# GpSimd's product of the states with C: one instruction for the three units of a group in place of three

## The chip, the cores and the metric
The kernel runs on one core of a Trainium2 chip. The metric is device time in microseconds (us), the median of some runs. The engines are named as the profile names them: PE (TensorE; PEld its weight loads), DVE (VectorE), ACT (ScalarE), POOL (GpSimd) and SP (SyncE, which only issues DMAs here).

## What is computed
Sixteen images of 64x64 positions with 96 channels pass two layers, each added to its input: first an upsampling, two matrix products around a quadratic and a downsampling, then a selective scan over the 4096 positions of each image:

```python
dA  = jnp.exp(delta[..., None] * A)                  # 192 inner channels x 16 states
dBu = delta[..., None] * Bm[:, :, None, :] * xc[..., None]
def step(h, inp):
    dA_t, dBu_t, C_t = inp
    h = dA_t * h + dBu_t
    y = jnp.einsum('bdn,bn->bd', h, C_t)             # the states times C, summed over the states
    return (h, y)
y = ys + xc * D
y = y * silu(z)                                      # and then the output projection
```

Before each layer stands a group normalization, whose sums need the whole image.

## The kernel before
**Units, groups, chunks.** The 192 x 16 pairs of channel and state of an image are laid out as 24 units of 128 rows, and the 4096 positions as 8 chunks of 512 columns. Three units that share their four states make a group, so a chunk has 8 groups, an image 64, and the program 1024. The text writes group 3/6 for group 6 of chunk 3 of an image, counting from zero.

**One group goes round the engines.** PE spreads B over the rows into the single PSUM bank `pb` (`spread_b`, L847). DVE multiplies `rep_u` with it (L1135 for two units, L1138 for the third) and runs three scans, one for each unit, into `hs` (L1145). ACT has made their factors `av` (L1009). POOL multiplies each unit's states `hs` with C, `cs`, into `hc` (L1186), and after the third copies the last column of the three states to `state` (L1190), where the next chunk's scans begin. PE then sums `hc` over the states into `py` (`reduce`, L856, six matmul records); ACT copies `py` out (L1052) once for four groups. `hs` and `hc` hold six units, two groups. DVE's first scan of a group waits for the copy of two groups before (`pool_st`), and POOL's first product for PE's reduction of two groups before (`pe_red`).

**What else POOL does in a chunk.** Two additions and products on `xcs` (L1235, L1238), two subtractions that split B in bf16 parts (L1211 to `dbc`, L1215 to `bc`), and one product of two 512-column halves on `dlt` (L1223), which waits for a DMA that stores `dlt` first. They stand at unit counts given by `AT["pool"]`, each behind the unit's product where one stands. Small steps of the normalization (L1173, L1176) stand among them.

**The order around it.** Everything is written out by hand: each engine walks the same unit counts, with a lag for some (`LAG`). On PE, between the units, stand the steps of the other layer for later images (`level`, `even`) and the projections of the scan (`X` L811, `Z` L817, `DBC`, `DT`, `OUT`). `spread_b` of group g+1 stands at unit 3g+1, and `reduce` of group g at 3g+5, behind `spread_b` of group g+2 and ahead of that of g+3. Where PE has little to do, `warm` puts in matmuls without a use (L711). Fourteen images run the full plan of steps (one first and thirteen full), the last two a plan with less and less on PE. PE waits in `reduce` on the semaphore `pool_hc`, of which POOL raises one for each product:

```python
pe.wait_ge(pool_hc, count(pool_hc, G * NU + 3 * g + 3))   # NU = 24 units, NG = 8 groups a chunk
```

Of the kernel before, what the change touches and what calls it, by code (L numbers as in the profile page):

```python
# [9 lines left out]
ALU = mybir.AluOpType  # L10
# [11 lines left out]
T = 512  # L22
NC8 = L // T
NJ, NQ = DI // 32, DSTATE // 4
NU = NJ * NQ
NG = NU // 3
NHC, NAV, NHS = 6, 8, 6
XB_H = 8
LEAD = 2
# [6 lines left out]
AT = {  # L36
    "pe": dict(pb=1, red=5),
    "act": dict(xn=10, y=(18, 6), d=11, mid=23, batch=16),
    "dve": dict(),
    "pool": dict(u=23, bc=(18, 22), y=(17, 8)),  # L40
    "sp": dict(rd=(1, 2, 3, 4), ru=(7, 9, 11, 13), cs=(15, 16, 17, 18), dl=21, du=4, x1=21, out=23),
}
# [155 lines left out]
def build(nc, A):  # L198
    ctx = ExitStack()
    with ctx:  # L200
        def sb(name, shape, dt=F32):
            return ctx.enter_context(nc.sbuf_tensor(name, shape, dt))
# [4 lines left out]
        def sem(name):  # L207
            return ctx.enter_context(nc.semaphore(name))
# [77 lines left out]
        cs = sb("cs", [128, 2, NQ, T])  # L286
        av = sb("av", [128, NAV, T])
        hs = sb("hs", [128, NHS, T])
        hc = sb("hc", [128, NHC, T])
# [6 lines left out]
        state = sb("state", [128, NG, 3])  # L296
# [53 lines left out]
        pool_st = sem("pool_st")  # L350
        pool_hc = sem("pool_hc")
        pe_red = sem("pe_red")
# [21 lines left out]
        def tok(ap, s, t0_, n):  # L374
            v = ap[bass.ds(s, 1), t0_:t0_ + n, :].rearrange("o t c -> (o t) c")
            return v.rearrange("(i p) c -> p i c", p=128)
# [107 lines left out]
        def count(sm, v):  # L484

            return max(v, 0)

        def ahead(s, k):

            return (s, k + LEAD) if k + LEAD < NC8 else (s + 1, k + LEAD - NC8)  # L490
# [4 lines left out]
        def _(sp):  # L495
# [112 lines left out]
            def load_x1o(s, k):  # L608

                src = x1_d[bass.ds(s, 1), :, k * T:(k + 1) * T].rearrange("o c t -> (o c) t")  # L610
                sp.dma_start(x1o[:, :], src).then_inc(x1o_ld, 16)
# [20 lines left out]
            def c_part(st, k, n):  # L632
                G = st.s * NC8 + k
                at = AT["sp"]
                if not ((G < -1 or G + 1 >= NS * NC8)):

                    p = (k + 1) % 2
                    if n == at["du"]:
                        sp.wait_ge(pool_u, count(pool_u, G + 2))
                        sp.sem_inc(sp_passed, 1)  # L640
                        sp.dma_start(du_d[p].rearrange("(t p) f -> p t f", p=C), dlt[:, :, :]).then_inc(du_st, 16)
                    if n == at["rd"][0]:
                        sp.wait_ge(dl_st, count(dl_st, (G + 2) * 16))
                        sp.sem_inc(sp_passed, 1)
                        sp.wait_ge(act_a, count(act_a, G * NU))
                        sp.sem_inc(sp_passed, 1)
                    if n == at["ru"][0]:
                        sp.wait_ge(du_st, count(du_st, (G + 2) * 16))
                        sp.sem_inc(sp_passed, 1)
                        sp.wait_ge(dve_bu, count(dve_bu, G * NG))  # L650
                        sp.sem_inc(sp_passed, 1)
                    if n == at["cs"][0]:
                        sp.wait_ge(dc_st, count(dc_st, (G + 2) * 16))
                        sp.sem_inc(sp_passed, 1)
                        sp.wait_ge(pool_hc, count(pool_hc, G * NU))
                        sp.sem_inc(sp_passed, 1)
                    for r in range(4):
                        rows = slice(32 * r, 32 * r + 32)
                        if n == at["rd"][r]:
                            sp.dma_start(rep_d[rows, p], dl_d[p].rearrange("(j p) f -> p j f", p=32))\  # L660
                                .then_inc(rd_ld[p], 16)
                        if n == at["ru"][r]:
                            sp.dma_start(rep_u[rows, p], du_d[p].rearrange("(j p) f -> p j f", p=32))\
                                .then_inc(ru_ld[p], 16)
                        if n == at["cs"][r]:
                            src = dc_d[p].rearrange("(q r) f -> r q f", r=4)[r].partition_broadcast(32)
                            sp.dma_start(cs[rows, p], src).then_inc(cs_ld[p], 16)
                if n == at["out"] and not (G < 1):
                    i = st.at[("OUT", k)]
                    sp.wait_ge(cb_free[i % RING], st.freed(i))  # L670
                    sp.sem_inc(sp_passed, 1)
                    k1, s1 = (k - 1) % NC8, st.s + (k - 1) // NC8
                    sp.dma_start(tok(otok, s1, k1 * T, T), os_[:, :, :]).then_inc(out_st, 16)
                if n == at["out"] and k < NC8 and not (G < 0):

                    load_x1o(st.s, k)
# [13 lines left out]
        def _(pe):  # L690
# [158 lines left out]
            def reduce(s, k, g):  # L849
                G = s * NC8 + k  # L850
                hf, q = g // NQ, g % NQ
                pe.wait_ge(pool_hc, count(pool_hc, G * NU + 3 * g + 3))
                if q == 0:
                    pe.wait_ge(act_y, count(act_y, G * 2 + hf))
                for j in range(3):
                    mm = pe.matmul(py[32 * j:32 * j + 32, :], rsel[:, :], hc[:, (3 * g + j) % NHC, :],  # L856
                                   start=(q == 0), stop=(q == NQ - 1), skip_group_check=True)
                mm.then_inc(pe_red, 1)
# [292 lines left out]
        def _(pool):  # L1151
# [26 lines left out]
            def unit(s, k, n):  # L1178
                G = s * NC8 + k
                g = n // 3  # L1180
                if n == 0:
                    pool.wait_ge(cs_ld[k % 2], count(cs_ld[k % 2], s * (4 * 64) + (k // 2 + 1) * 64))
                if n % 3 == 0:
                    pool.wait_ge(pe_red, count(pe_red, G * NG + g + 1 - NHC // 3))
                pool.wait_ge(dve_h, count(dve_h, G * NU + n + 1))
                pool.tensor_tensor(hc[:, n % NHC, :], hs[:, n % NHS, :], cs[:, k % 2, g % NQ, :], ALU.mult)\  # L1186
                    .then_inc(pool_hc, 1)
                if n % 3 == 2:

                    pool.tensor_copy(state[:, g, :], hs[:, n % NHS - 2:n % NHS + 1, T - 1]).then_inc(pool_st, 1)  # L1190

            def a_part(st, k, n):
                if n in AT["pool"]["bc"]:

                    s2, k2 = ahead(st.s, k)
                    G2 = s2 * NC8 + k2

                    if st.s >= 0:
                        pool.wait_ge(pool_hc, count(pool_hc, (G2 - LEAD) * NU + n + 1))
                        if n % 3 == 2:  # L1200
                            pool.wait_ge(pool_st, count(pool_st, (G2 - LEAD) * NG + n // 3 + 1))
                        if n == AT["pool"]["y"][0]:
                            pool.wait_ge(pool_g, count(pool_g, (G2 - LEAD) * 2 + 1))
                    else:
                        pool.wait_ge(pool_s, count(pool_s, 4))
                        pool.wait_ge(pool_u, count(pool_u, G2))
                    if n == AT["pool"]["bc"][0]:
                        i = st.at[("DBC", k)]
                        pool.wait_ge(cb_free[i % RING], st.freed(i))

                        pool.tensor_tensor(dbc[64:64 + DSTATE, :], dbc[0:DSTATE, :], bc3[0:DSTATE, k2 % 4, :], ALU.subtract)\  # L1211
                            .then_inc(pool_bc, 1)
                    else:
                        pool.wait_ge(act_mid, count(act_mid, G2 + 1))
                        pool.tensor_tensor(bc3[32:32 + DSTATE, k2 % 4, :], dbc[64:64 + DSTATE, :],  # L1215
                                           bc3[64:64 + DSTATE, k2 % 4, :], ALU.subtract).then_inc(pool_bc, 1)
                    pool.wait_ge(pool_bc, count(pool_bc, G2 * 2 + 1 + AT["pool"]["bc"].index(n)))
                if n == AT["pool"]["u"]:
                    s2, k2 = ahead(st.s, k)
                    G2 = s2 * NC8 + k2  # L1220

                    pool.wait_ge(dl_st, count(dl_st, (G2 + 1) * 16))
                    pool.tensor_tensor(dlt[:, :, :], dlt[:, :, :], xcs[:, k2 % 4], ALU.mult).then_inc(pool_u, 1)  # L1223
# [85 lines left out]
```

## Time and profile before

| | us |
|---|---|
| median of 3 runs (6271.82 to 6277.77) | 6276.55 |
| the profiled execution's own time | 6274.24 |
| its span in the profile | 6272.4 |
| PE busy in it | 6018.2 (96%) |
| DVE busy in it | 5612.7 (89%) |
| POOL busy in it | 5210.9 (83%) |
| ACT busy in it | 5098.6 (81%) |
| granted clock of PE, mean | 0.969 |

Busy time counts the instructions' records, so the matmuls of `warm` count as well, and a busy PE is not PE at its peak.

### The profile page before, as it was taken

Reading aid. Unit: us, or ns where it says so; the run is one execution under the profiler, and the core shown is the slowest. Engines: PE = TensorE matmul, PEld = TensorE weight load, DVE = VectorE, ACT = ScalarE, POOL = GpSimd, SP = SyncE. Lnnn points to the kernel's source line nnn. Section 1 sums busy time; section 2 is a strip of 40 time slices with the busy share of each in tenths; the row PEclk is TensorE's granted clock in tenths of the full one; section 3 lists DMA queues with packets and bytes.
Section 4 is the critical chain, followed back from the end, with each engine's and each line's share of the span. In section 5 each row is a group of like instructions: output and inputs, shape, how many; then the busy total and the mean of one; then the engine's idle time right before and its main releaser. Section 6 shows DMA issues by size and latency. Waiting matters only on the chain. (4 is left out here: it accounts for less than half of the span.)

```text
span 6272.4 us, 101148 instructions
## 1 busy us (share of the span) xinstructions
PE 6018.2 (96%) x32260; PEld 3119.1 (50%) x32260; DVE 5612.7 (89%) x5483; ACT 5098.6 (81%) x8658; POOL 5210.9 (83%) x5092
## 2 busy tenths in 40 slices
PE   8999999999999999999999999999999999999876
PEld 5645545455454555555454554545545455554322
DVE  0089999999999999999999999999999999999998
ACT  4578888888888888888888888888888888887765
POOL 0078888888888888888888888888898888899998
PEclk9999999999999999999999999999999999998666
DMA  3367676676767767676676767667686676767563
GB/s 95 89 162 172 161 168 159 162 169 161 181 145 169 163 159 175 157 175 152 164 169 162 172 156 169 155 164 172 154 184 146 165 169 160 171 150 162 135 141 76
DMA packets 805842, 983.38 MB, mean 157 GB/s; under 512 B 391258, under 2 KB 417542, under 8 KB 805318
## 3 DMA queue, kind: packets, MB, share of 16 engines
q1 hardware_dynamic: 805318, 976.92, 66.5%
q8 instruction: 265, 4.34, 0.3%
q14 instruction: 259, 2.12, 0.1%
HBM read 717.71 MB, written 259.00 MB: 156 GB/s over the span
## 5 line engine op out<-in xcount | busy, mean ns | idle before, releaser
L1186 POOL TENSOR_TENSOR hc<-hs,cs 128x512 f32<-128x512 f32 x3072 | 3838.0, 1273 | 614.6 <-PE py L856 316.7
L1145 DVE TENSOR_TENSOR_SCAN hs<-av,state,b 128x512 f32<-128x512 f32 x2688 | 3256.5, 1260 | 17.9 <-POOL state L1190 11.2
L1009 ACT ACTIVATE av<-rep_d,nega 128x512 f32<-128x512 f32 x3072 | 2096.1, 713 | 26.5 <-DVE hs L1145 21.8
L1135 DVE TENSOR_TENSOR b<-rep_u,pb 128x1024 f32<-128x1024 f32 x1024 | 1247.2, 1218 | 283.3 <-PE pb L847 278.0
L856 PE MATMUL py<-hc,rsel 128*32 128x512 f32 x6144 | 1136.1, 631 | 88.8 <-POOL hc L1186 83.0
L770 PE MATMUL cb<-xu,w1a 96*128 96x392 f32 x2400 | 982.0, 512 | 10.4 <-ACT g L957 6.2
L775 PEld LDWEIGHTS cb<-w2c,g 128*98 128x98 f32 x9600 | 884.6, 167 | 169.9 <-issue 107.0
L775 PE MATMUL cb<-w2c,g 128*98 128x96 f32 x9600 | 909.4, 251 | 17.5 <-ACT g L957 9.3
L957 ACT ACTIVATE g<-cb,b1a 128x392 f32<-128x392 f32 x1200 | 679.9, 580 | 87.0 <-PE cb L770 79.1
L811 PE MATMUL cb<-xn,wtap 96*96 96x512 f32 x1536 | 725.0, 608 | 8.4 <-ACT xcs L983 6.3
L1138 DVE TENSOR_TENSOR b<-rep_u,pb 128x512 f32<-128x512 f32 x1024 | 702.1, 686 | 0.0
L770 PEld LDWEIGHTS cb<-xu,w1a 96*128 96x128 f32 x2400 | 414.2, 191 | 398.2 <-issue 200.3
L1145 DVE TENSOR_TENSOR_SCAN hs<-av,zero_state,b 128x512 f32<-128x512 f32 x384 | 466.7, 1261 | 3.5 <-ACT av L1009 3.5
L847 PE MATMUL pb<-bc,selb 96*128 96x512 bf16 x1024 | 405.1, 396 | 64.7 <-DVE b L1138 64.6
L950 ACT ACTIVATE vr<-cb 98x384 f32<-98x384 f32 x400 | 195.3, 488 | 316.7 <-PE cb L775 314.9
L811 PEld LDWEIGHTS cb<-xn,wtap 96*96 96x96 f32 x1536 | 244.1, 166 | 409.3 <-issue 384.1
L856 PEld LDWEIGHTS py<-hc,rsel 128*32 128x32 f32 x6144 | 157.0, 109 | 506.8 <-POOL hc L1186 243.4
L1223 POOL TENSOR_TENSOR dlt<-dlt,xcs 96x1024 f32<-96x1024 f32 x128 | 302.3, 2362 | 75.9 <-DMA delta_scratch<-dlt 75.9
L764 PE MATMUL cb<-up_h,t1r 128*96 128x196 f32 x1600 | 344.9, 338 | 7.8 <-DMA t1r<-t_scratch 7.8
L838 PE MATMUL cb<-wo,xcs 96*128 96x96 f32 x2048 | 342.8, 293 | 3.9 <-POOL xcs L1238 3.6
L1238 POOL TENSOR_TENSOR xcs<-xcs,zs 96x512 f32<-96x512 f32 x256 | 324.4, 1267 | 20.1
L838 PEld LDWEIGHTS cb<-wo,xcs 96*128 96x128 f32 x2048 | 293.2, 206 | 83.1 <-issue 45.6
(110 smaller groups left out, 6806.5 us busy)
## 6 DMA issues: line engine op xcount, KB each, us to landing
rep_d<-delta_scratch SPq DMA_DIRECT2D x512, 384.0 KB, 7.1
rep_u<-deltax_scratch SPq DMA_DIRECT2D x512, 384.0 KB, 6.3
cs<-c_scratch SPq DMA_DIRECT2D x512, 256.0 KB, 6.0
delta_scratch<-dlt SPq DMA_DIRECT2D x128, 384.0 KB, 3.1
deltax_scratch<-dlt SPq DMA_DIRECT2D x128, 384.0 KB, 9.0
t1r<-t_scratch SPq DMA_DIRECT2D x160, 240.0 KB, 6.6
v_scratch<-v2s SPq DMA_DIRECT2D x192, 192.0 KB
xb<-in_x SPq DMA_DIRECT2D x128, 192.0 KB, 4.7
```

The lines of the kernel that those rows point to most:

```text
L770: mm = pe.matmul(bank[:, 0:BC], w1a[:, 128 * f:128 * f + 128], xu[:, b % 2, :], start=True, stop=True)
L775: mm = pe.matmul(bank[0:GH, C * j:C * j + C], g2[:, b % 2, f, GH * j:GH * j + GH], w2c[:, f, :], start=(f == 0), stop=(f == NF - 1))
L811: mm = pe.matmul(bank[0:C, :], wtap[:, tap, t, :], xn[:, k2 % 2, tap:tap + T], start=(tap == 0), stop=(tap == 2))
L838: pe.matmul(o, xcs[:, p, t, tb], wo[:, t, :], start=(t == 0), stop=False)
L847: pe.matmul(pb[:, :], selb[:, g % NQ, :], bc3[:, k % 4, :], start=True, stop=True).then_inc(pe_b, 1)
L856: mm = pe.matmul(py[32 * j:32 * j + 32, :], rsel[:, :], hc[:, (3 * g + j) % NHC, :], start=(q == 0), stop=(q == NQ - 1), skip_group_check= ...
L957: act.activation(g2[:, b % 2, f, :], bank[:, 0:BC], ACT.Square, bias=b1a[:, f:f + 1]).then_inc(fr, 1)
L1009: act.activation(av[:, n % NAV, :], rep_d[:, k % 2, j, :], ACT.Exp, scale=nega[:, q, j:j + 1])\
L1135: dve.tensor_tensor(b3[:, 0:2, :], rep_u[:, k % 2, 3 * hf:3 * hf + 2, :], pb[:, None, :].broadcast_to([128, 2, T]), ALU.mult).then_inc(dve ...
L1138: dve.tensor_tensor(b3[:, 2, :], rep_u[:, k % 2, 3 * hf + 2, :], pb[:, :], ALU.mult).then_inc(dve_bu, 1)
L1145: dve.tensor_tensor_scan(hs[:, n % NHS, :], av[:, n % NAV, :], b3[:, n % 3, :], start, ALU.mult, ALU.add)\
L1186: pool.tensor_tensor(hc[:, n % NHC, :], hs[:, n % NHS, :], cs[:, k % 2, g % NQ, :], ALU.mult)\
```

## The change
The three products of a group become one instruction of 1536 columns. It is issued at the group's third unit, with C read three times over (a broadcast in the middle of the access pattern), and so it waits for the third scan. `pool_hc` counts groups, and its three readers (SP's load of `cs`, PE's `reduce`, POOL's own subtractions) count so too.

```diff
@@ sp: c_part
-                        sp.wait_ge(pool_hc, count(pool_hc, G * NU))
+                        sp.wait_ge(pool_hc, count(pool_hc, G * NG))
@@ pe: reduce
-                pe.wait_ge(pool_hc, count(pool_hc, G * NU + 3 * g + 3))
+                pe.wait_ge(pool_hc, count(pool_hc, G * NG + g + 1))
@@ pool: unit
-                if n % 3 == 0:
-                    pool.wait_ge(pe_red, count(pe_red, G * NG + g + 1 - NHC // 3))
+                if n % 3 != 2:
+                    return
+                h, p = n % NHS - 2, n % NHC - 2
+                pool.wait_ge(pe_red, count(pe_red, G * NG + g + 1 - NHC // 3))
                 pool.wait_ge(dve_h, count(dve_h, G * NU + n + 1))
-                pool.tensor_tensor(hc[:, n % NHC, :], hs[:, n % NHS, :], cs[:, k % 2, g % NQ, :], ALU.mult)\
-                    .then_inc(pool_hc, 1)
-                if n % 3 == 2:
-
-                    pool.tensor_copy(state[:, g, :], hs[:, n % NHS - 2:n % NHS + 1, T - 1]).then_inc(pool_st, 1)
+                pool.tensor_tensor(hc[:, p:p + 3, :], hs[:, h:h + 3, :],
+                                   cs[:, k % 2, g % NQ, None, :].broadcast_to([128, 3, T]), ALU.mult).then_inc(pool_hc, 1)
+                pool.tensor_copy(state[:, g, :], hs[:, h:h + 3, T - 1]).then_inc(pool_st, 1)
@@ pool: a_part
-                        pool.wait_ge(pool_hc, count(pool_hc, (G2 - LEAD) * NU + n + 1))
-                        if n % 3 == 2:
-                            pool.wait_ge(pool_st, count(pool_st, (G2 - LEAD) * NG + n // 3 + 1))
-                        if n == AT["pool"]["y"][0]:
+                        pool.wait_ge(pool_hc, count(pool_hc, (G2 - LEAD) * NG + (n + 1) // 3))
+                        pool.wait_ge(pool_st, count(pool_st, (G2 - LEAD) * NG + (n + 1) // 3))
+                        if n == AT["pool"]["bc"][0]:
                             pool.wait_ge(pool_g, count(pool_g, (G2 - LEAD) * 2 + 1))
```

The order of the rows on PE, DVE, ACT and SP is the same in both kernels. On POOL, from the work on `xcs` behind group 5 of a chunk to the copy behind group 0 of the next, there stood:

```order
L1238 TENSOR_TENSOR xcs<-xcs,zs 96x512
L1186 TENSOR_TENSOR hc<-hs,cs 128x512
L1211 TENSOR_TENSOR dbc<-dbc,bc 16x512
L1186 TENSOR_TENSOR hc<-hs,cs 128x512 x2
L1190 COPY state<-hs 128x3
L1186 TENSOR_TENSOR hc<-hs,cs 128x512 x2
L1215 TENSOR_TENSOR bc<-dbc,bc 16x512
L1186 TENSOR_TENSOR hc<-hs,cs 128x512
L1190 COPY state<-hs 128x3
L1223 TENSOR_TENSOR dlt<-dlt,xcs 96x1024
L1186 TENSOR_TENSOR hc<-hs,cs 128x512 x3
L1190 COPY state<-hs 128x3
```

In the same place of POOL's program there now stands (the lines behind L1188 are shifted up by one):

```order
L1237 TENSOR_TENSOR xcs<-xcs,zs 96x512
L1210 TENSOR_TENSOR dbc<-dbc,bc 16x512
L1188 TENSOR_TENSOR hc<-hs,cs 128x1536
L1190 COPY state<-hs 128x3
L1214 TENSOR_TENSOR bc<-dbc,bc 16x512
L1188 TENSOR_TENSOR hc<-hs,cs 128x1536
L1190 COPY state<-hs 128x3
L1222 TENSOR_TENSOR dlt<-dlt,xcs 96x1024
L1188 TENSOR_TENSOR hc<-hs,cs 128x1536
L1190 COPY state<-hs 128x3
```

The first subtraction has moved ahead of the whole product of group 6, where one unit's product stood before it, and the second ahead of that of group 7, where two stood.

At group 4/0 of an image POOL's program has the two steps of the next image's normalization (`gnx`) behind the copy. Before:

```order
L1186 TENSOR_TENSOR hc<-hs,cs 128x512 x3
L1190 COPY state<-hs 128x3
L1173 TENSOR_TENSOR gnx<-ve,mhalf 96x1
L1176 TENSOR_TENSOR gnx<-mg,gnx 96x1
L1186 TENSOR_TENSOR hc<-hs,cs 128x512 x3
L1190 COPY state<-hs 128x3
```

And now:

```order
L1188 TENSOR_TENSOR hc<-hs,cs 128x1536
L1190 COPY state<-hs 128x3
L1173 TENSOR_TENSOR gnx<-ve,mhalf 96x1
L1176 TENSOR_TENSOR gnx<-mg,gnx 96x1
L1188 TENSOR_TENSOR hc<-hs,cs 128x1536
L1190 COPY state<-hs 128x3
```

Nothing has moved there but the products themselves.

## Rows read from the trace of the kernel before

**Rows 1.** Windows: busy us and instructions by engine, PEclk, DMA share, GB/s.

```profile
347.00:5600.00 5253.00, 5176.57 (x28367) 2692.91 (x28366) 4925.27 (x4790) 4458.90 (x7603) 4573.70 (x4465) 1.00 0.70 164
5600.00:6272.00 672.00, 536.47 (x2118) 220.75 (x2116) 646.92 (x623) 459.40 (x717) 615.86 (x601) 0.74 0.57 130
...
3131.60:3152.60 21.00, 19.24 (x125) 10.68 (x122) 21.00 (x22) 15.33 (x31) 20.61 (x22) 1.00 0.82 160
```

**Rows 2.** Waits of PE, 347 to 5600 us: us in total, times, longest.

```profile
PE py L856 <- POOL hc L1186: 27.8, 55, 0.8
```

**Rows 3.** Timeline of PE, two stretches of one image: start, us, instruction [idle before].

```profile
3056.43 1.06 PE L856 MATMUL py<-hc,rsel 128*32 128x512 f32 x6 [0.16 <-POOL hc L1186]
...
3140.82 1.06 PE L856 MATMUL py<-hc,rsel 128*32 128x512 f32 x6 [0.59 <-POOL hc L1186]
...
3144.65 0.39 PE L847 MATMUL pb<-bc,selb 96*128 96x512 bf16 x1
...
3146.95 1.06 PE L856 MATMUL py<-hc,rsel 128*32 128x512 f32 x6 [0.80 <-POOL hc L1186]
...
3151.54 1.06 PE L856 MATMUL py<-hc,rsel 128*32 128x512 f32 x6 [0.36 <-POOL hc L1186]
```

**Rows 4.** Timeline of DVE in the same stretch.

```profile
3133.19 3.62 DVE L1145 TENSOR_TENSOR_SCAN hs<-av,state,b 128x512 f32<-128x512 f32 x3
...
3147.26 1.22 DVE L1135 TENSOR_TENSOR b<-rep_u,pb 128x1024 f32<-128x1024 f32 x1
```

**Rows 5.** Timeline of POOL in the same stretch, groups 3/5 (its copy) to 4/1.

```profile
3127.79 0.20 POOL L1190 COPY state<-hs 128x3 f32<-128x3 f32 x1
...
3130.52 1.27 POOL L1186 TENSOR_TENSOR hc<-hs,cs 128x512 f32<-128x512 f32 x1
3131.87 1.15 POOL L1211 TENSOR_TENSOR dbc<-dbc,bc 16x512 f32<-16x512 f32 x1
3133.10 2.49 POOL L1186 TENSOR_TENSOR hc<-hs,cs 128x512 f32<-128x512 f32 x2
3135.54 0.18 POOL L1190 COPY state<-hs 128x3 f32<-128x3 f32 x1
3135.68 2.51 POOL L1186 TENSOR_TENSOR hc<-hs,cs 128x512 f32<-128x512 f32 x2
3138.28 1.15 POOL L1215 TENSOR_TENSOR bc<-dbc,bc 16x512 bf16<-16x512 f32 x1
3139.50 1.27 POOL L1186 TENSOR_TENSOR hc<-hs,cs 128x512 f32<-128x512 f32 x1
3140.71 0.19 POOL L1190 COPY state<-hs 128x3 f32<-128x3 f32 x1
3140.86 2.36 POOL L1223 TENSOR_TENSOR dlt<-dlt,xcs 96x1024 f32<-96x1024 f32 x1
3143.18 3.72 POOL L1186 TENSOR_TENSOR hc<-hs,cs 128x512 f32<-128x512 f32 x3
3146.83 0.20 POOL L1190 COPY state<-hs 128x3 f32<-128x3 f32 x1
...
3151.43 0.18 POOL L1190 COPY state<-hs 128x3 f32<-128x3 f32 x1
```

**Rows 6.** Single lines over the whole trace: duration in ns, least/median/most, first and last start.

```profile
L1186 POOL TENSOR_TENSOR hc<-hs,cs x3072: 1253/1272/1327, 335.5 to 6256.9; 128x512 f32<-128x512 f32 x192
...
L1223 POOL TENSOR_TENSOR dlt<-dlt,xcs x128: 2342/2361/2383, 304.1 to 6176.8; 96x1024 f32<-96x1024 f32 x128
...
L1145 DVE TENSOR_TENSOR_SCAN hs<-av,state,b x2688: 1242/1255/1282, 385.5 to 6255.4; 128x512 f32<-128x512 f32 x192
```

**Rows 7.** Waits of DVE, 5840 to 6250 us (columns as in rows 2).

```profile
DVE b L1135 <- PE pb L847: 5.1, 8, 1.6
```

**Rows 8.** Timeline of PE, a chunk of the last images, and the last reduction.

```profile
5888.93 1.93 PE L856 MATMUL py<-hc,rsel 128*32 128x512 f32 x6 [1.07 <-POOL hc L1186]
...
6258.20 1.56 PE L856 MATMUL py<-hc,rsel 128*32 128x512 f32 x6 [0.59 <-POOL hc L1186]
```

## Prediction

> **What bounds the kernel now.** I first cut the span in windows. From 347 to 5600 us, which is the fourteen images with the full plan, PE is busy 5176.6 of 5253 us at a granted clock of 1.00, DVE 4925.3, POOL 4573.7 [rows 1]. PE is the pace there; it idles 76.4 us in all. So I asked what PE waits for in that stretch: 27.8 us, in 55 waits, it is POOL's product (reduction L856 behind L1186) [rows 2]. That is 2.0 us and four waits an image, and it is the most that the change could give there if every such wait went. Next I looked where in an image they lie. One is early, at group 2/0: 0.16 us at 3056.43. The other three stand together, at groups 3/7, 4/0 and 4/1: 0.59, 0.80 and 0.36 us [rows 3]. In that short stretch the roles are turned: DVE is busy for 21.00 of 21.00 us, POOL 20.61, PE only 19.24 [rows 1]. DVE sets the groups' spacing, 5.24 us, POOL has more than its share to do between two groups, and PE, which has caught up, waits for POOL. Everywhere else in the image PE comes to a reduction after its product is done, and so has no wait there.
>
> The last two images, from 5600 us on, have little on PE, whose granted clock is 0.74 in the mean; DVE is busy 646.9 of 672 us [rows 1] and sets the time, with eight short waits for PE's `pb`, 5.1 us, from 5840 to 6250 [rows 7].
>
> **The one instruction.** No row has a product of 1536 columns. A product of 512 takes 1272 ns and one of two halves of 512 takes 2361 [rows 6], so 512 columns more cost 1.09 us. By start to start, which is what the next instruction sees: one product to the copy behind it 1.21 us (3139.50 to 3140.71), three products 3.65 (3143.18 to 3146.83), the product of 1024 columns to the next 2.32 (3140.86 to 3143.18) [rows 5]. So the fused one occupies 1.21 + 2 x 1.09 = 3.39, or 1.21 + 2 x (2.32 - 1.21) = 3.43; I take 3.40. The bounds are 2.18 below (the two further parts alone, no fixed part: excluded as far as any row goes, kept as the end) and 3.65 above (nothing saved; C read three times over and three rows of the pattern could cost that). The saving is 0.25 us a group, where the three ran back to back.
>
> By the reported durations the three would have cost 3 x 1.272 = 3.82 and the fused one 1.272 + 2.18 = 3.45, a saving of 0.36. The Trainium skill, Perfetto Trace Analysis, section GPSIMD Engine Instruction, says that such durations don't compose and that one should time this engine by start-to-start spacing. The rows bear that out, since the next record starts 0.04 to 0.07 us before the one ahead of it ends; by the durations the delays worked out below would be 0.4 to 0.5 us an image smaller.
>
> **What it saves on POOL is not on the path; what it adds is.** Before, the first two products ran under the second and third scan, and after the third scan one product of 1.27 us was left. Now the whole 3.40 us begins where the third product began. The `hc` of a group is later by 3.40 - 1.21, that is 2.18 us, if POOL had been waiting for scans. PE doesn't notice this in most of an image, since it comes later than that. It does in the stretch with the three waits, and I follow it there [rows 5]:
> - The copy behind group 3/5 goes from 3127.79 to 3129.97 (+2.18).
> - From that copy to the products of 4/0 (3143.18) POOL has no gap, 15.39 us. Of this the products of groups 3/6 and 3/7 are 1.35 (3130.52 to 3131.87) + 2.44 (3133.10 to 3135.54) + 2.60 (3135.68 to 3138.28) + 1.21 = 7.60. Two fused ones are 6.80, and the two subtractions, which now follow a completion that POOL itself waits for, I charge with 0.1 each (1.35 against 1.21 is such a wait): 7.00. So the product of 4/0 starts at +2.18 - 0.60 = +1.58, at 3144.76. The scans of its group were done long before then, and those of 3/6, which end at 3136.81 less 5.24 [rows 4], were done before its product too (3134.0): POOL runs without a gap.
> - The product of 4/0 ends at +1.58 - 0.25 = +1.33, that of 4/1 (copy at 3151.43) at +1.33 - 0.25 = +1.08.
> - PE starts the reduction of 4/0 1.33 later, at 3148.3. It needs 4.2 us to be ready for that of 4/1 (3151.54 less its wait of 0.36 less 3146.95 [rows 3]), so it is ready at 3152.5, and the product is there at 3152.5: the reduction starts about 1.06 later.
> - DVE is not held up inside the stretch: the `pb` that PE makes at 3144.65 is wanted at 3147.26 [rows 3, 4], a cover of 2.2 us, and PE is late by 1.5 at most there. Without that cover the delay would be the same 1 us again.
> - The first subtraction is 1.0 later, and ACT's copy of its result waits for it; PE is waiting for POOL anyway at that time.
>
> From 4/1 on PE has no further wait for POOL up to 2/0 of the next image, and is the pace, so the 1.06 us stay: 14 x 1.06 = +14.8 us. At 2/0 the product starts when a DMA lets `dlt` go, and a fused one ends 0.25 earlier, so that PE's wait of 0.16 there goes: 13 x 0.16 = -2.1.
>
> **The last two images.** Each chunk there has the same POOL lag, and PE waits at group x/1, 1.07 us at 5888.93, at a reduction that takes 1.93 in place of 1.06 [rows 3, 8]; behind it stands `X`, and behind that the `pb` for which DVE has its waits [rows 7]. A delay of 1.06 comes to DVE in full where DVE waits now and less what slack there is elsewhere: about seven chunks, +7 us (bounds 0 and 8 x 1.06 = 8.5). The very last reduction waits for POOL as well [rows 8], with nothing to cover it: +2.2.
>
> **Sum.** 14.8 - 2.1 + 7 + 2.2 = +21.9 us on the profiled 6274.24 (span 6272.4 and 1.8 around it). The median is 2.3 above that execution, so I put 6276.55 + 21.9 = 6298 us, 0.35% slower. About 0.2%, 12.5 us, is what a measurement of this kernel can tell from no change.
>
> **The rivals.**
> - *The delay is swallowed.* PE idles 76.4 - 27.8 = 48.6 us for other things than POOL in the long stretch [rows 1, 2], 3.5 an image. If these waits have their own clock (a DMA, say) and not PE's, they take up the 1.06 of each image. Left: 7 + 2.2 - 2.1 = +7, or 6284, no change that can be told. Against it: most waits behind ACT there are for work that PE itself handed out. The same comes out if the fused instruction takes some 3.25. 0.20.
> - *Faster: the fused instruction is cheap.* The delay at 4/1 is 1.06 less five times what it falls below 3.40, so that it is gone at 3.19 us. At 3.0, the reduction of 4/0 would be 1.33 - 1.6 = -0.27, and that of 4/1, which PE can reach 0.36 earlier than now, -0.63: 14 x -0.63 - 2.1, the last images -4, the end +1.8: -13, 6263. Only a fixed part far above what the rows of 512 and 1024 columns give would do it. 0.06.
> - *No saving: the pattern costs 3.65.* Then +1.33 at 4/0 becomes +2.3, and so does 4/1 in about the same measure: 14 x 2.3 + 12 + 2.4 = +47, 6323. 0.08.
> - *The clock.* PE now waits about 1.9 us ahead of the reduction of 3/6, where it had none. In the last images, where it waits like that again and again, its granted clock falls to the lower level, 1.2 GHz, and the six records of L856 take 1.93 for 1.06 [rows 1, 3, 8]. If it fell there once in each image, the 4.6 us of work up to the next reduction would take 3.7 more: some +52, to 6350. Against it: the waits of 0.80 us in the stretch leave it at 1.00 [rows 1, 3]. 0.07.
> - *The port.* The Trainium skill, SBUF — State Buffer, section Who interferes with whom, says that GpSimd and a DVE instruction with two SBUF inputs exclude each other for a whole instruction, whichever starts first; DVE's scan reads `av` and, as one column, `state`. In this trace scans lie beside products all the time and take 1242 to 1282 ns, the products 1253 to 1327 [rows 6], so nothing is shut out; if the longer product shut a scan out even once a group, by its 2.18 us more, it would cost up to 1024 x 2.18 = 2230 us, 8500 in all. 0.01.
>
> **How the numbers follow.** The forecast, +21.9 with 13 to 35 around it, has 0.58. The time is that of this case. Slower: 0.58 + 0.08 + 0.07 + 0.01 = 0.74; the same 0.20; faster 0.06. The range goes from 6275, which leaves out the fast case and part of the swallowed one, up to 6330, above the case without a saving.
>
> **What would show it.** Right: L1188 at about 3.46 us, copy 3.40 behind its start; POOL busy about 250 us less; PE's waits for `hc` from 347 to 5600 us grown from four an image to five or six, with a new one of some 1.9 us at 3/6, in all about 27.8 + 14 = 42 us; DVE's waits for `pb` after 5840 us from 5.1 to about 12; group 4/0's reduction 6.1 us behind its third scan. Wrong: L1188 under 3.2 us or over 3.6; waits grown like that with an image's length unchanged (swallowed); a granted clock below 1.00 in the long stretch.

## The result, and the profile after

| | before | after |
|---|---|---|
| median, us | 6275.78 (6271.82 to 6277.77, 4 runs) | 6312.32 (6307.97 to 6314.12, 4 runs) |
| span of the profiled execution, us | 6272.4 | 6306.2 |
| granted clock of PE, mean | 0.969 | 0.962 |

The ratio is 1.0055, with a 95% interval of 1.0043 to 1.0067: the change costs 0.55%, 36.5 us by the medians and 33.8 by the two profiled executions. Forecast were 6298 us, in a range of 6275 to 6330.

The page of after begins with the busy time of each engine.

```profile
PE 6035.5 (96%) x32260; PEld 3125.7 (50%) x32260; DVE 5617.5 (89%) x5483; ACT 5095.2 (81%) x8658; POOL 4921.3 (78%) x3044
```

POOL is busy 290 us less than before (5210.9). So the instruction does what it is meant to do, on an engine whose busy time wasn't the price. Two single lines over the whole trace (least, median and most in ns) answer to [rows 6]:

```profile
L1188 POOL TENSOR_TENSOR hc<-hs,cs x1024: 3412/3451/3478, 336.2 to 6288.1; 128x1536 f32<-128x1536 f32 x171
...
L1145 DVE TENSOR_TENSOR_SCAN hs<-av,state,b x2688: 1242/1255/1282, 384.2 to 6286.7; 128x512 f32<-128x512 f32 x192
```

The fused product is 3451 ns in the median, and the scans that run beside it are to the nanosecond what they were.

The windows (columns as in [rows 1]): the two long stretches, then 21 us of an image from 2016 us on, and 21 us of another from 3140 us on.

```profile
347.00:5600.00 5253.00, 5170.61 (x28255) 2688.55 (x28253) 4908.22 (x4770) 4436.42 (x7570) 4301.59 (x2656) 1.00 0.70 163
5600.00:6306.00 706.00, 561.35 (x2218) 230.82 (x2215) 669.49 (x643) 478.13 (x749) 600.21 (x366) 0.74 0.57 128
...
2016.00:2037.00 21.00, 18.16 (x116) 10.25 (x118) 21.00 (x22) 14.37 (x29) 20.37 (x15) 1.00 0.81 156
...
3140.00:3161.00 21.00, 19.11 (x118) 10.67 (x113) 20.16 (x21) 13.68 (x27) 20.32 (x14) 0.92 0.77 151
```

Both hold the groups from 3/6 on to about 4/1 (the second begins 0.97 us further ahead of its reduction of 3/6; the 21 us from 3140.97 have the same 0.92 and 20.16). In the first all is as forecast: DVE busy throughout, the clock at 1.00. In the second the mean clock is 0.92, and DVE has lost 0.84 us. Where, the finer windows of the second image show, the wait ahead of the reduction of 3/6, the 3.2 us behind it, and the 1.8 behind those:

```profile
3144.56:3146.44 1.88, 0.00 (x1) 0.00 (x1) 1.88 (x2) 1.85 (x5) 1.88 (x2) 0.94 0.02 4
3146.44:3149.60 3.16, 3.16 (x14) 1.24 (x15) 3.16 (x4) 1.98 (x4) 2.95 (x3) 0.50 0.82 212
3149.60:3151.40 1.80, 1.80 (x10) 0.65 (x8) 1.33 (x2) 0.00 (x0) 1.80 (x2) 1.00 0.78 197
```

PE, busy until then, waits 1.88 us; behind the wait its granted clock is 0.50, the 1.2 GHz level, and 3.4 us after it fell it is back at 1.00. The clock's own records have such a fall in 12 of the 14 images, from 0.3 us ahead of the end of that wait to 1.5 behind it, each of 3.41 us (one more lies at 5221.5); before had none from 347 to 5600 us. The same 3 us in the image of 2016 us, behind a wait as long, read 1.00:

```profile
2021.47:2024.60 3.13, 3.13 (x21) 1.41 (x21) 3.13 (x4) 1.98 (x4) 2.92 (x3) 1.00 0.86 196
```

What PE waits for from 347 to 5600 us; the first row answers to [rows 2]:

```profile
PE py L856 <- POOL hc L1188: 28.2, 18, 1.9
PE cb L811 <- ACT xcs L983: 9.6, 14, 0.7
PE cb L738 <- DMA xb<-in_x: 9.5, 11, 2.1
```

The total for POOL is nearly what it was, 28.2 for 27.8 us, and an image is longer all the same: a sum of waits doesn't say where an engine stands. PE's reductions, first in the image without a fall of the clock, then in the one with it (timeline of PE; answers to [rows 3]):

```profile
2021.47 0.63 PE L856 MATMUL py<-hc,rsel 128*32 128x512 f32 x3 [1.88 <-POOL hc L1188]
...
2026.39 1.06 PE L856 MATMUL py<-hc,rsel 128*32 128x512 f32 x6 [0.34 <-POOL hc L1188]
...
2032.25 1.06 PE L856 MATMUL py<-hc,rsel 128*32 128x512 f32 x6 [0.54 <-POOL hc L1188]
```
```profile
3146.44 1.07 PE L856 MATMUL py<-hc,rsel 128*32 128x512 f32 x3 [1.89 <-POOL hc L1188]
...
3152.49 1.06 PE L856 MATMUL py<-hc,rsel 128*32 128x512 f32 x6
...
3157.75 1.06 PE L856 MATMUL py<-hc,rsel 128*32 128x512 f32 x6
```

With the fall (second fence) PE comes to 3/7 and 4/0 later than the product does, so its waits there are gone, but the reduction of 3/7 starts 6.05 us after that of 3/6 in place of 4.92. And DVE, which the forecast left untouched, is now held up there (timeline of DVE):

```profile
3151.77 1.23 DVE L1135 TENSOR_TENSOR b<-rep_u,pb 128x1024 f32<-128x1024 f32 x1 [0.84 <-PE pb L847]
```

POOL in the same stretch, from the product of 3/5 to the copy of 4/1 (answers to [rows 5]):

```profile
3135.34 3.44 POOL L1188 TENSOR_TENSOR hc<-hs,cs 128x1536 f32<-128x1536 f32 x1 [2.02 <-DVE hs L1145]
3138.72 0.19 POOL L1190 COPY state<-hs 128x3 f32<-128x3 f32 x1
...
3141.72 1.15 POOL L1210 TENSOR_TENSOR dbc<-dbc,bc 16x512 f32<-16x512 f32 x1 [0.23 <-POOL xcs L1237]
3142.95 3.44 POOL L1188 TENSOR_TENSOR hc<-hs,cs 128x1536 f32<-128x1536 f32 x1
3146.32 0.19 POOL L1190 COPY state<-hs 128x3 f32<-128x3 f32 x1
...
3153.72 3.44 POOL L1188 TENSOR_TENSOR hc<-hs,cs 128x1536 f32<-128x1536 f32 x1
3157.11 0.18 POOL L1190 COPY state<-hs 128x3 f32<-128x3 f32 x1
...
3161.42 0.18 POOL L1190 COPY state<-hs 128x3 f32<-128x3 f32 x1
```

The copy starts 3.37 to 3.39 us behind the product. From the copy of 3/5 to that of 4/1 it is now 22.70 us, before 23.64 (3127.79 to 3151.43).

**The last images.** DVE's waits for `pb` from 5840 to 6284 us, which answer to [rows 7], and then one chunk: group x/5 on POOL and PE, and DVE's first product of the next chunk.

```profile
DVE b L1135 <- PE pb L847: 12.7, 18, 1.0
```
```profile
6059.86 3.43 POOL L1188 TENSOR_TENSOR hc<-hs,cs 128x1536 f32<-128x1536 f32 x1 [2.08 <-DVE hs L1145]
...
6063.35 1.93 PE L856 MATMUL py<-hc,rsel 128*32 128x512 f32 x6 [1.25 <-POOL hc L1188]
6065.20 1.17 PE L838 MATMUL cb<-wo,xcs 96*128 96x96 f32 x4
...
6070.43 0.63 PE L847 MATMUL pb<-bc,selb 96*128 96x512 bf16 x1
...
6071.16 1.23 DVE L1135 TENSOR_TENSOR b<-rep_u,pb 128x1024 f32<-128x1024 f32 x1 [0.96 <-PE pb L847]
```

PE waits 1.25 us for the late product of x/5, works through `OUT` (L838, L839) at half clock, and only then spreads B for the next chunk; DVE waits 0.96 us for it.

**Where the 33.8 us are.** I took the start of every reduction and the end of every third scan from both traces and subtracted. Up to the end of 0/7 of the fifteenth image PE's reductions have lost 21.5 us (the scans there 21.2): 24.6 between the reductions of 3/5 and 4/2, which is called the stretch below (1.72 to 1.88 in the twelve images with a fall of the clock, 1.19 and 1.21 in the two without), less 3.5 in the groups at 2/0, plus 1.7 in all at the ends of images, where the two traces differ by -1.3 to +3.1 each time, less 1.3 ahead of the first of these stretches. From there to the last scan 10.2 more are lost, and behind it 2.4.

### The profile page after: what moved, and what is told of

The parts are those of the page before. It is cut to its first block and busy times, and to the rows that moved or that the text cites. A ratio compares the mean times of both kernels' runs of the same rounds, so it can differ in the third digit from the quotient of the medians.

```text
span 6306.2 us, 98974 instructions
## 1 busy us (share of the span) xinstructions
PE 6035.5 (96%) x32260; PEld 3125.7 (50%) x32260; DVE 5617.5 (89%) x5483; ACT 5095.2 (81%) x8658; POOL 4921.3 (78%) x3044
## 5 line engine op out<-in xcount | busy, mean ns | idle before, releaser
L1188 POOL TENSOR_TENSOR hc<-hs,cs 128x1536 f32<-128x1536 f32 x1024 | 3532.6, 3450 | 918.4 <-DVE hs L1145 892.2
L1009 ACT ACTIVATE av<-rep_d,nega 128x512 f32<-128x512 f32 x3072 | 2094.9, 713 | 20.5 <-DVE hs L1145 15.7
L856 PE MATMUL py<-hc,rsel 128*32 128x512 f32 x6144 | 1144.1, 635 | 133.2 <-POOL hc L1188 129.5
L775 PE MATMUL cb<-w2c,g 128*98 128x96 f32 x9600 | 909.3, 251 | 16.9 <-ACT g L957 8.8
L856 PEld LDWEIGHTS py<-hc,rsel 128*32 128x32 f32 x6144 | 157.4, 110 | 551.7 <-issue 329.6
L838 PE MATMUL cb<-wo,xcs 96*128 96x96 f32 x2048 | 342.9, 293 | 3.7 <-POOL xcs L1237 3.5
L838 PEld LDWEIGHTS cb<-wo,xcs 96*128 96x128 f32 x2048 | 293.3, 206 | 85.1 <-issue 47.9
```

Of the source, the lines that this page charges most:

```text
L775: mm = pe.matmul(bank[0:GH, C * j:C * j + C], g2[:, b % 2, f, GH * j:GH * j + GH], w2c[:, f, :], start=(f == 0), stop=(f == NF - 1))
L838: pe.matmul(o, xcs[:, p, t, tb], wo[:, t, :], start=(t == 0), stop=False)
L1009: act.activation(av[:, n % NAV, :], rep_d[:, k % 2, j, :], ACT.Exp, scale=nega[:, q, j:j + 1])\
L1188: pool.tensor_tensor(hc[:, p:p + 3, :], hs[:, h:h + 3, :], cs[:, k % 2, g % NQ, None, :].broadcast_to([128, 3, T]), ALU.mult).then_inc(poo ...
```

## The experiments

The rows of each kernel are numbered by its own source, so that `reduce` is L856 or L858 and the products L1186 to L1196. The first four shared their runs of the kernel before (median 6277.99 of 21), the last three theirs (6274.3 of 21).

**wait_alone: the late start without the fusion.** Three products again, all issued behind the third scan.

```diff
-                pool.tensor_tensor(hc[:, p:p + 3, :], hs[:, h:h + 3, :],
-                                   cs[:, k % 2, g % NQ, None, :].broadcast_to([128, 3, T]), ALU.mult).then_inc(pool_hc, 1)
+                for j in range(3):
+                    pool.tensor_tensor(hc[:, p + j, :], hs[:, h + j, :], cs[:, k % 2, g % NQ, :], ALU.mult).then_inc(pool_hc, 1)
```

> The three products stay separate instructions of 512 columns, but all three wait for the group's third scan, in the order of the changed kernel: the wait without the saving. If the lateness of hc behind the third scan is what costs (theory), this is slower than the changed kernel: group 3/5's copy comes 2.43 us later than before instead of 2.18, nothing is won back on the way to 4/1, and the reduction of 4/0 starts about 2.3 us later than before in each image: 14 x 2.3 = 32 us, some 9 for the clock that falls at 3/6, 17 in the last images and 2.4 at the end, together about +60 us on the kernel before, 6335. If the long instruction itself (1536 columns, C read three times over) were the cost (rival), it would be near the kernel before, 6276, or at least faster than the changed one, 6312.

Measured: 6343.99 us (6341.39 to 6348.23), ratio 1.0105 [1.0088, 1.0121]. PE's waits from 347 to 5600 us, and the first of them in one image:

```profile
PE py L856 <- POOL hc L1189: 42.8, 40, 2.8
```
```profile
3155.03 0.63 PE L856 MATMUL py<-hc,rsel 128*32 128x512 f32 x3 [2.46 <-POOL hc L1189]
```

An image loses 2.3 to 2.5 us in the stretch 3/5 to 4/2 (four lose 2.6 to 3.7; in three of these the clock is at the lower level for 6.8 us), and nothing comes back at 2/0. The time is 9 us above the 6335 expected, on the side of the theory; most of the 9 lies in the last two images, which lose 25.5 us by the third scans where 17 were expected. So the cost of the change is the later start: alone it takes 66.0 us, and the change, with the fusion, 36.5, which is 29.5 less.

**warm8: after, and PE kept at work ahead of the wait.** Eight matmuls without a use ahead of the reduction of 3/6, in the time in which PE would idle.

```diff
-    return padded(rows + (warm(rows) if kind != "tail" else []))
+    return padded(rows + (warm(rows) + [(94, ("WARM", 94, i)) for i in range(8)] if kind != "tail" else []))
```

> The changed kernel with eight more matmuls without a use in each of the fourteen full images, placed just ahead of the reduction of group 3/6, where PE now idles 1.9 us: 8 x 0.215 = 1.7 us of work in that gap. 
Measured: 6298.43 us (6295.91 to 6303.12), ratio 1.0031 [1.002, 1.0043]. Its reductions of 3/6 (in its pieces) and 3/7:

```profile
3143.24 0.63 PE L856 MATMUL py<-hc,rsel 128*32 128x512 f32 x3
...
3148.18 1.06 PE L856 MATMUL py<-hc,rsel 128*32 128x512 f32 x6 [0.35 <-POOL hc L1188]
```
```profile
3133.00:3154.00 21.00, 20.09 (x118) 10.07 (x114) 21.00 (x22) 14.71 (x26) 20.40 (x13) 1.00 0.78 149
```

The second fence is the windows' row around these groups; it has the clock at 1.00 and DVE at 21.00 again (20.98 in the 21 us from 3137.77, which lie about the wait as those from 2016 us do). There is no fall of the clock in the whole stretch up to 5600 us, and each of the 14 images loses 1.19 to 1.22 us in the stretch. So the fall costs up to 0.67 us in an image that has it, 24.6 - 14 x 1.21 = 7.7 us in all. The profiled spans differ by 9.4, the medians by 13.9; of the 9.4, what is above 7.7 lies at the ends of images and in the last two, where traces scatter (its last two images lose 12.6). The 6303 expected was met, 5 us below.

**split5: after, with three products in group 5 of each chunk.** Only the group whose late copy begins POOL's gapless row is as before.

```diff
+FUSED = (0, 1, 2, 3, 4, 6, 7)
...
+                if g not in FUSED:
+                    if n % 3 == 0:
+                        pool.wait_ge(pe_red, count(pe_red, G * NG + g + 1 - NHC // 3))
+                    pool.wait_ge(dve_h, count(dve_h, G * NU + n + 1))
+                    pool.tensor_tensor(hc[:, n % NHC, :], hs[:, n % NHS, :], cs[:, k % 2, g % NQ, :], ALU.mult).then_inc(pool_hc, 1)
```

> The changed kernel with three separate products again in group 5 of each chunk alone; the other seven groups keep the one instruction. Theory: the whole loss of the long stretch comes from the late copy behind group 5, at which the row of POOL's work without a gap begins. With it gone, the products of 3/6, 3/7, 4/0 and 4/1 end 0.35, 0.33, 0.55 and 0.57 us earlier than in the kernel before, PE's waits there shrink from 1.8 to some 1.2 us an image, and its clock does not fall: -8 us, -2 at group 2/0, about +2 for group 1 in the last images, +2 at the end: -6 against the kernel before, 6270, and PE's clock at 1.00 in the long stretch. Rival, that each fused group adds its own share of the loss: 7/8 of +36, 6308.

Measured: 6276.38 us (6271.47 to 6284.27), ratio 0.9997 [0.9988, 1.0007]. The whole loss is gone, which refutes the rival of 6308. The gain that I expected, 6 us, is inside the interval by the time; in the stretch of the trace it isn't there. Two rows of PE behind 4/1 in one image show where it went:

```profile
3154.31 0.93 PE L772 MATMUL cb<-xu,w1a 96*128 96x392 f32 x2 [0.34 <-DVE b1a L1123]
...
3155.94 2.82 PE L813 MATMUL cb<-xn,wtap 96*96 96x512 f32 x6 [0.49 <-ACT xcs L985]
```

The reduction of 4/1 is 0.60 us earlier than before; that of 4/2 is not earlier at all (0.00 to 0.02 in every image). In between PE meets a small DVE step of the normalization, `b1a`, and then ACT's copy of `X`, `xcs`. The wait for `b1a` is new (4.1 us from 347 to 5600 us, none before), and behind its two records 0.02 us of the lead is left. The wait for `xcs` stood there before, 0.47 us in this image: `xcs` comes when it came, however early PE is.

**lag_only: one instruction in groups 6, 7 and 0 alone**, where POOL runs without a gap: FUSED = (0, 6, 7) in the diff above.

> One instruction only in groups 6, 7 and 0 of a chunk, where POOL is behind and the scans are done before it comes to the product; three separate ones in groups 1 to 5, where POOL waits for scans. Theory (one instruction gains where POOL is behind and loses where it waits for scans): in each image 0.55 us less wait at 4/1, 14 x 0.55 = -8, -2 at group 2/0, about -3 in the last images, nothing at the end: -13 against the kernel before, 6263. Rival (each fused group costs its share): 3/8 of +36, 6290.

Measured: 6275.71 us (6273.1 to 6284.25), ratio 0.9998 [0.9989, 1.0008]. PE's waits for POOL from 347 to 5600 us have shrunk from 27.8 to 15.7 us (11.5 for the fused products, L1196, and 4.2 for the separate ones, L1189), and the time has not moved: neither the 6263 expected nor the 6290 of the rival.

```profile
PE cb L740 <- DMA xb<-in_x: 11.7, 10, 2.4
PE py L858 <- POOL hc L1196: 11.5, 28, 0.5
...
PE cb L772 <- DVE b1a L1123: 5.0, 14, 0.4
PE py L858 <- POOL hc L1189: 4.2, 14, 0.3
```

The reduction of 4/1 is 0.62 us earlier, that of 4/2 0.00; the same two waits stand behind it. What is won at 2/0 (3.6 us in all, 3.9 in split5) doesn't show in the time either: PE's waits for the DMA of `xb`, 7.4 us before, are 11.7 here and 11.8 in split5. Whether they take it up or only scatter, no run tells.

**five_only: the kernel before, with one instruction in group 5 alone**: FUSED = (5,), the subtractions in their old places.

> The kernel before with the one instruction in group 5 of each chunk alone, and everything else as it was, the places of the two subtractions too. Theory (the loss is the 2.18 us by which the copy behind group 5 is late, and the other fused groups only give a part of it back): nothing is given back, so the products up to 4/1 stay 2.2 us late, and an image takes about 2.3 us longer: 14 x 2.3 = 32, the last images some 20, nothing at the very end: +52 on the kernel before, 6329, which is more than with all eight groups fused (6312). Rival (each fused group costs its share): 1/8 of +36, 6282.

Measured: 6329.59 us (6327.33 to 6345.14), ratio 1.009 [1.0076, 1.0104]. Expected were 6329. One group of eight fused costs more than all eight: 1.83 to 2.01 us in the stretch in twelve images (3.2 and 3.4 in two, whose clock is at the lower level for 6.8 us), since the products behind it make up for nothing. It also settles whether the subtractions, which the change moved ahead, are the cause: here they stand in their old places, and the loss is there; in split5 they are moved, and there is none. Its wait at 3/6 in one image:

```profile
3152.88 0.63 PE L858 MATMUL py<-hc,rsel 128*32 128x512 f32 x3 [2.02 <-POOL hc L1189]
```

**early_only: the kernel before, with a smaller lag for two small steps on DVE.** `DG` (`cst`, L1124) and `WG` (`b1a`, L1121) each add a bias. The edit asks for both two units earlier, but DVE takes its steps from one list in order, and a step whose predecessor is not yet due stays where it was.

```diff
-            run(lambda row: row[0] + LAG["bn" if row[1][0] in ("ST", "D_hi") else "dve"], unit, step, lambda st, k, n: None, lambda st, k, n: None, finish)
+            run(lambda row: row[0] + (1 if row[1][0] in ("DG", "WG") else LAG["bn" if row[1][0] in ("ST", "D_hi") else "dve"]), unit, step, lambda st, k, n: None, lambda st, k, n: None, finish)
```

> The kernel before with three separate products, and one other thing changed: DVE does its two small steps of the normalization, DG and WG, two units earlier in its order (a lag of 1 in place of 3). Where three separate products came earlier at 4/1 (the two kernels with a part of the groups fused), PE lost its lead again within 10 us to two waits, one for DVE's b1a (0.34 us) and one for ACT's xcs (0.49). ACT had lost 2.8 us to DVE's step DG before. If that is where the lead goes (theory), PE's wait for xcs of 0.47 us an image goes in the kernel before too: 14 x 0.47 = -6.6, 6271. If DVE's and ACT's scan work sets these waits whatever the order of the small steps (rival): 6278.

Measured: 6273.03 us (6267.84 to 6281.35), ratio 0.9995 [0.9986, 1.0004]: by the time, nothing can be told, not between the 6271 expected and no effect either. DVE's rows in one image show that only one of the two steps has moved:

```profile
3145.80 2.44 DVE L1145 TENSOR_TENSOR_SCAN hs<-av,state,b 128x512 f32<-128x512 f32 x2
3148.16 0.12 DVE L1124 TENSOR_TENSOR cst<-cb,cbase 96x1 f32<-96x1 f32 x1
...
3156.35 1.27 DVE L1145 TENSOR_TENSOR_SCAN hs<-av,state,b 128x512 f32<-128x512 f32 x1
...
3158.12 0.14 DVE L1121 TENSOR_TENSOR b1a<-cb,b1t 128x3 f32<-128x3 f32 x1
3158.18 2.44 DVE L1145 TENSOR_TENSOR_SCAN hs<-av,state,b 128x512 f32<-128x512 f32 x2
```

`cst` stands behind the second scan of 4/1, before behind the third; `b1a` stands behind the first scan of 4/3, as before, in all fourteen images. So this run and the next test `cst` alone. An image is 0.14 to 0.19 us shorter in the stretch, and one wait is, which was 6.3 us before:

```profile
PE cb L811 <- ACT xcs L983: 3.8, 14, 0.3
```

**lag_early: lag_only and early_only together.**

> One instruction in groups 6, 7 and 0 alone, and DVE's steps DG and WG two units earlier. Theory: the 0.6 us that the earlier products of 4/1 gain are no longer lost to the waits for b1a and xcs, and the 0.47 of the latter goes as well: 14 x (0.6 + 0.47) = -15, with -0.3 an image at 2/0 another -4: 6259, the first version that beats the kernel before. Rival (the lead is lost to the next wait all the same): 6275.

Measured: 6266.86 us (6261.84 to 6269.76), ratio 0.9985 [0.9976, 0.9993]. Expected were 6259. This is the one version that beats the kernel before, by 7.4 us; its interval stays below 1. Every image is 0.72 to 0.73 us shorter in the stretch, of the 1.07 expected; the wait for `b1a` is left:

```profile
3141.33 1.06 PE L858 MATMUL py<-hc,rsel 128*32 128x512 f32 x6 [0.37 <-POOL hc L1189]
...
3146.60 0.93 PE L772 MATMUL cb<-xu,w1a 96*128 96x392 f32 x2 [0.35 <-DVE b1a L1123]
```

That wait is 5.0 us from 347 to 5600 us, the same as in lag_only; that for `xcs`, 6.8 us in lag_only, is no longer among PE's waits. Each of the two edits alone gave nothing that the time shows, 0.00 and 0.16 us an image.

## Why the prediction was right, and where it was off

**The one instruction, 3.40 us from start to copy.** Right: 3.37 to 3.41 in the stretch. That the three rows of the pattern or C read over three times cost something (the rival of 6323) is out. The start-to-start spacing was the right price: with the reported durations the delays would have been 0.4 to 0.5 us smaller, some 0.6 at 4/1; the images without a fall of the clock lost 1.1 there. To that extent this trace agrees with the Trainium skill, Perfetto Trace Analysis, section GPSIMD Engine Instruction, which has this engine timed by spacing.

**The copy of 3/5 later by 2.18, POOL's row shorter by 1.10.** Each a little less, with the sum as forecast. Behind its third scan the copy went from 1.48 to 3.53 us, +2.05 and not +2.18, since POOL had not been waiting for that scan: now a product of 3.38 begins 0.15 behind the scan, before one of 1.21 began 0.26 behind it. The row shrank by 0.95: the second subtraction and the first now wait 0.14 and 0.23 for POOL's own completion, where I had charged 0.1 each. So +1.10 at 4/1, forecast +1.08.

**The reductions.** In the two images at full clock they start +1.92, +1.66, +1.39 and +1.11 later at 3/6, 3/7, 4/0 and 4/1, forecast +1.33 and +1.06 for the last two. The reduction of 4/0 starts 6.3 us behind its third scan in these images and 6.8 to 7.0 in the others, 4.9 before; forecast was 6.1. Up to 4/2 another 0.1 comes, as PE's wait for ACT's `xcs` (in warm8 7.8 us from 347 to 5600 us, before 6.3). From there to 2/0 of the next image nothing is given back within an image: between 0/7 and 1/7 the two traces agree to 0.01 us. The swallowed delay (0.20, 6284) is refuted: PE's other waits within an image take up nothing of a delay. Those at the ends of images, for the DMA of `xb`, may be; they went both ways by up to 3 us and added up to 1.7.

**The steady term, 14 x 1.06 = 14.8, was mis-sized,** and so was the reason given against *the clock* as a rival. It measured 24.6. Of this 14 x 1.21 = 16.9 is the mechanism, as warm8 shows, and 7.7 the clock. I had asked whether the clock falls or not, put a chance of 0.07 on it and a price of 3.7 us an image, 52 in all. It fell in 12 of 14 images, at the very place named, for 3.4 us, and cost up to 0.67: at half clock PE loses 1.7 us in 3.4, but in these images its waits at 3/7, 4/0 and 4/1 would have been 0.34 + 0.54 + 0.08 = 0.96 anyway, and 1.7 - 0.96 = 0.74. I had taken the whole length for lost, although the same text had PE waiting for POOL right behind. The argument against it (waits of 0.80 leave the clock alone) was about waits less than half as long. A granted clock below 1.00 in the long stretch was among the signs of being wrong, and it came: on the clock the forecast failed, while its mechanism held. The step "DVE is not held up inside the stretch" holds without a fall (21.00 of 21.00 us busy) and not with one (0.84 us idle). The count of waits followed: 18 in 28.2 us, not five or six an image in 42.

**At 2/0, 13 x 0.16 = -2.1:** -3.5 measured, -0.17 to -0.35 an image. Small, and the right sign.

**The last images, +7:** 10.2 measured, and by another place. I followed x/1, `X` and the `pb` behind it. The rows show x/5: product, reduction, `OUT`, `pb` of x/0, at half clock, with nothing between that could take up the delay, and DVE waiting 0.96 us for it. DVE's waits rose to 12.7 us, about the 12 forecast, which alone wouldn't have shown that the place was wrong. In the last image the third scans lose 9.9 us, against before. Each of its eight chunks loses 1.07 us at group x/0 (the first 1.16), as in five_only; in split5, where group 5 is split and the others are not, no chunk loses anything there, and the image gains 1.4. So it is group 5 here too. The image before the last can't be read like that: it loses 0.2 us in the changed kernel and 5.2 in early_only, which touches no product. That a chunk's loss, 1.07, is near the 1.06 forecast for one is luck, since the place was another.

**The end, +2.2:** +2.0 to the start of the last reduction, +2.4 to the end of the span.

**The ceiling.** I wrote that 27.8 us, PE's waits for POOL, is the most that the change could give there. split5 and lag_only took away about half of that wait (13.6 and 15.7 us are left) and gained nothing in the stretch, since the next steps of PE wait for DVE's `b1a` (4.1 and 5.0 us, none before) and ACT's `xcs` (6.9 and 6.8 us, 6.3 before), which don't follow PE. A delay is paid in full and a lead isn't: that was not in the working, and it is why the fast rival (6263) could not have come at the 3.0 us that it asked for. lag_early shows that the place of `cst` on DVE held back the larger part: with it one scan earlier the wait for `xcs` goes, and two thirds of what I counted on stay (0.73 of 1.07).

**The port (0.01)** is out: scans of 1242 to 1282 ns beside products of 3.45 us. Nothing of the kind that the Trainium skill, SBUF — State Buffer, section Who interferes with whom, leads one to fear shows here.

**Open.** Why two images of fourteen keep their clock behind a wait as long; what sets the scatter at the ends of images; and what holds back the last 0.35 us in lag_early. The order of DVE, in which `b1a` stands behind a scan there, is the likely cause and was not tried, since no run moved `b1a`.

## What to carry to other kernels

Merging instructions saves the merged engine some time (here 0.25 us in 3.65) and gives up the overlap of its first parts with their producer: ask at each consumer how late the *last* element comes, and follow it where the engine has no gap to catch up in. Merge where the instructions already run back to back, and leave them apart where they follow a producer; but a lead is worth something only as far as the next wait, so look for that one before you count it. A new wait on TensorE can have two prices, its own and that of the clock behind it, and here the second only counted for what PE would not have idled anyway. And look in the trace whether an edit moved what it was meant to move: a smaller lag left `b1a` where it was.

## What the runs showed that I had not expected

- A single wait of 1.9 us, in a stretch in which PE is otherwise busy at a granted clock of 1.00, is followed by 3.4 us at 1.2 GHz in 12 of 14 images (in 11 behind the 2.0 us of five_only, in 13 behind the 2.5 us of wait_alone, some of these for 6.8 us). The waits of 0.80 us of before had no such effect in any. Eight matmuls (1.9 us) in the place of the wait keep the clock at 1.00 and take 7.7 us off.
- One fused group of eight is slower (1.009) than eight (1.0055), and three are as fast as none (0.9998): the order of the three doesn't follow the count of merged instructions.
- A product of 1536 columns with C broadcast over the middle costs what the plain ones of 512 and 1024 extrapolate to: 3.37 to 3.41 us from start to start for 3.39 to 3.43.
